# Layernorm statistics at the producers, an output projection by four tiles, a store by four tiles, and first counts ahead of the next turns, in a two-attention, two-MoE kernel on one core

## The reference

```
x = x + attn_a(layernorm(x), Wq, Wkv, Wout, bout, rel_emb)   # 16 heads of 64, one key/value head, relative bias, causal
x = x + ffn(layernorm(x), router_w, w1, b1, w2, b2)          # 8 experts, top 1, capacity 256
x = x + attn_b(layernorm(x), ...)                            # 16 heads of 8, causal, gated by a geometric score; ends in out @ out_w + out_b
x = x + ffn(layernorm(x), the same weights)
```

## Time and profile before

| | |
|---|---|
| runs | 1184.18 us median of 3 (1183.88 to 1186.83) |
| profiled execution | 1186.11 us, span 1184.40 us, mean granted PE clock 0.915 |
| PE, DVE, ACT, POOL busy | 85%, 64%, 51%, 28% of the span |
| attention A | about 36 to 583.7 us |
| moe1 | 583.9 to 665.6 us |
| b_ln, geometry, prepare_b | 665.9 to 777 us |
| attention B | 777 to 1082 us |
| out_b (`project_out`) | 1082.2 to 1093.6 us |
| moe2 | 1093.9 to 1176.5 us |
| store | to 1184.4 us |

### The profile page before, as it was taken

How to read it: one execution, slowest core, us unless ns; L and a number is a source line. 1 busy time by engine, 2 the same in 40 slices (tenths; PEclk the granted TensorE clock), 3 DMA queues, 4 the chain that set the end, 5 groups by cost and what they waited for, 6 DMA issues and landing times. The chain is left out here.

```text
span 1184.4 us, 18918 instructions
## 1 busy us (share of the span) xinstructions
PE 1006.3 (85%) x6474; PEld 651.5 (55%) x6474; DVE 761.2 (64%) x2007; ACT 598.5 (51%) x1179; POOL 328.1 (28%) x418
## 2 busy tenths in 40 slices
PE   4589999999989999999739367789999999997483
PEld 2457666676667666676439234355544445544372
DVE  5177766767567756777533599777777777763522
ACT  2477666666567666766213254314555555555120
POOL 0422112211122112210053206443443333421522
PEclk9799999999999999999959689878999999998587
DMA  5630000000000000000151100000000000000613
GB/s 176 150 88 1 1 1 1 1 2 1 1 1 1 1 1 1 1 1 1 40 175 46 46 0 1 1 1 1 1 2 1 1 2 1 1 1 3 192 56 90
DMA packets 47615, 32.40 MB, mean 27 GB/s; under 512 B 9104, under 2 KB 43680, under 8 KB 47520
## 3 DMA queue, kind: packets, MB, share of 16 engines
q1 hardware_dynamic: 45472, 26.93, 8.0%
q0 software_dynamic: 2048, 4.26, 1.1%
HBM read 21.59 MB, written 11.69 MB: 28 GB/s over the span
## 5 line engine op out<-in xcount | busy, mean ns | idle before, releaser
L891 DVE TENSOR_REDUCE attn_b_least<-attn_b_slot 128x1 f32<-128x512 f32 (+3 forms) x384 | 195.0, 552 | 64.5 <-PE attn_b_slot L809 43.8
L622 ACT ACTIVATE attn_a_prob<-attn_a_score,attn_a_m_all 128x128 f32<-128x128 f32 (+7 forms) x256 | 188.8, 740 | 65.5 <-DVE attn_a_m_all L544 62.3
L958 ACT ACTIVATE attn_b_probT<-attn_b_st 128x1024 f32<-128x1024 f32 (+1 forms) x192 | 145.2, 808 | 149.9 <-PE attn_b_st L833 148.5
L540 DVE TENSOR_REDUCE attn_a_m_far<-attn_a_score 128x1 f32<-128x512 f32 (+3 forms) x192 | 105.6, 550 | 71.7 <-PE attn_a_score L451 60.9
L463 PE MATMUL attn_a_slot<-tab,attn_a_prob 128*128 128x128 f32 x1152 | 151.6, 276 | 0.0
L807 PE MATMUL attn_b_slot<-KS,attn_b_alone 128*128 128x512 f32 (+2 forms) x384 | 147.4, 454 | 3.2 <-POOL attn_b_alone L980 2.4
L475 PE MATMUL attn_a_o<-attn_a_ptsb,Vd 128*64 128x512 f32 x288 | 142.3, 613 | 0.0
L475 PE MATMUL attn_a_o<-attn_a_ptsa,Vd 128*64 128x512 f32 x288 | 142.2, 612 | 0.0
L463 PEld LDWEIGHTS attn_a_slot<-tab,attn_a_prob 128*128 128x128 f32 x1152 | 134.3, 142 | 10.7 <-issue 3.2
L807 PEld LDWEIGHTS attn_b_slot<-KS,attn_b_alone 128*128 128x128 f32 x384 | 74.8, 205 | 86.1 <-DVE attn_b_least L891 52.5
L631 ACT ACTIVATE attn_a_ptsa<-attn_a_slot 128x512 f32<-128x512 f32 x144 | 85.7, 595 | 69.8 <-PE attn_a_slot L463 69.3
(11 more groups left out here) (223 smaller groups left out, 1857.3 us busy)
## 6 DMA issues: line engine op xcount, KB each, us to landing
moe_weights_w<-in_L_ffn_w_dram SPq DMA_DIRECT2D x32, 256.0 KB, 5.0
to_experts<-xn SPq DMA_DIRECT2D x2, 1056.0 KB, 9.0
moe_experts_xe<-to_experts SPq DMA_DIRECT2D x16, 132.0 KB, 2.6
bias_by_query_and_key<-bias_by_distance SPq DMA_DIRECT2D x2, 1024.0 KB
bias_near<-bias_by_query_and_key SPq DMA_DIRECT2D x2, 1024.0 KB, 8.1
from_experts<-xn SPq DMA_DIRECT2D x2, 1024.0 KB, 9.6
moe_experts_back<-from_experts SPq DMA_DIRECT2D x8, 256.0 KB, 3.8
moe_weights_b<-in_L_ffn_b_dram SPq DMA_DIRECT2D x16, 64.0 KB, 5.4
```

What stands on the lines that cost most here:

```text
L540: nc.vector.tensor_reduce(least, score[t % 2][:, at:at + nk - win], AX.X, ALU.min).then_inc(far_done, 1)
L622: nc.scalar.activation(probs(g)[:, j, 0:nk], score[t % 2][:, at:at + nk], ACT.Exp, bias=m_all[:, j:j + 1], scale=-1.0, accum_out=rowsum[g ...
L891: nc.vector.tensor_reduce(least[m // PER % 2][:, c, a, qt:qt + 1], bank[u % SLOTS_S][:, 0:w], AX.X, ALU.min).then_inc(slot_free, 1)
L958: nc.scalar.activation(probT[n % 2][:, two, lo:], st[:, two, lo:], ACT.Exp, scale=-1.0).then_inc(exp_done, 1)
```

## The change

Five edits. (1) `bn_stats` leaves `b_ln` and both `dispatch` phases. Each tile's statistics are made where X gets its last value: in `attention_a` behind the add with `s = 1`, in moe1's `experts` behind each chunk's four adds, in `project_out` behind each chunk's add. They go to one tile `stats` that lives through the program. Each has a wait on the add before it on the same engine. `a_ln` keeps its own. (2) `dispatch`'s parts are now eight and eight tiles, and DVE's order around the first chunk changes. (3) On PE `counts(0)` stands in front of `turn(1)`. (4) `project_out` works by chunks: four transposes into one bank, one copy, four matmuls, one add, with a buffer for each chunk; out_b is added to X by POOL inside `attention_b`, batch 0 at step 0 and batch 1 at step 12. (5) The final store is four DMAs, issued by SP inside moe2's `experts` as each chunk is updated; the last phase only waits.

```
 def dispatch(...):
-        parts = (range(0, BLK), range(BLK, TILES))
+        parts = (range(0, 2 * BLK), range(2 * BLK, TILES))
...
             turn(0)
             logits(0)
+            counts(0)
             turn(1)
-            counts(0)
...
-            statistics(range(0, BLK))
             variance(0)
             nc.vector.tensor_scalar(xn[:, :, D].bitcast(I32), spare[:, :], -(SLOTS + 1.0), None, ALU.add)
-            statistics(range(BLK, 2 * BLK))
             inverse(0)
             normal(0)
-            statistics(range(2 * BLK, TILES))
             variance(1)
+            normal(1)
+            inverse(1)
             choose(0)
-            inverse(1)
-            normal(1)
             place(0)
             normal(2)
             normal(3)
...
 def attention_a, add(g):
                 nc.vector.tensor_tensor(x, x, bank[u % SLOTS_S][:, 0:P], ALU.add).then_inc(added, 1)
+                if s:
+                    dve.wait_ge(added, g + 1)
+                    nc.vector.bn_stats(stats[:, b * QT + tile(g), :], x)
...
 def attention_b, POOL:
+                if n in (0, PER):
+                    bias_out(n // PER)
...
+            def bias_out(b):
+                mine = X[:, b * QT:(b + 1) * QT, :]
+                nc.gpsimd.tensor_tensor(mine, mine, boutb[:, :].unsqueeze(1).to_broadcast([P, QT, D]), ALU.add)
...
 def project_out(...):
+            turn(0)
+            turn(1)
+            for c in range(NC):
+                project(c)
+                if c + 2 < NC:
+                    turn(c + 2)
...
+            for c in range(NC):
+                tiles = slice(c * BLK, (c + 1) * BLK)
+                dve.wait_ge(y_done, c + 1)
+                nc.vector.tensor_tensor(X[:, tiles, :], X[:, tiles, :], y_ps[c][:, :, :], ALU.add).then_inc(summed, 1)
+                dve.wait_ge(summed, c + 1)
+                for i in range(c * BLK, (c + 1) * BLK):
+                    nc.vector.bn_stats(stats[:, i, :], X[:, i, :])
...
 def experts(...), SP:
+            if out is not None:
+                into, stored = out
+                for i in range(TILES // BLK):
+                    tiles = slice(i * BLK, (i + 1) * BLK)
+                    sp.wait_ge(updated, i + 1)
+                    sp.dma_start(into.rearrange("b (t p) d -> p (b t) d", p=P)[:, tiles, :], X[:, tiles, :]).then_inc(stored, 16)
 def experts(...), DVE:
+            for c in range(TILES // BLK):
+                dve.wait_ge(fetched[c], 16)
+                for i in range(c * BLK, (c + 1) * BLK):
+                    ins = nc.vector.scalar_tensor_tensor(X[:, i, :], back[:, i, :], gate[:, i:i + 1], X[:, i, :], ALU.mult, ALU.add)
+                ins.then_inc(updated, 1)
+                if out is None:
+                    dve.wait_ge(updated, c + 1)
+                    for i in range(c * BLK, (c + 1) * BLK):
+                        nc.vector.bn_stats(stats[:, i, :], X[:, i, :])
```

More of the change, by code:

```diff
@@ L103, in _ @@
             nc.vector.memset(xnT[:, :, 0:1], 0.0)
-            for i in range(TILES):
-                ins = nc.vector.bn_stats(stats[:, i, :], X[:, i, :])
-            link(ins)
+            if made is None:
+                for i in range(TILES):
+                    ins = nc.vector.bn_stats(stats[:, i, :], X[:, i, :])
+                link(ins)
             for i in range(TILES):
@@ L228, in wide @@
                 return x.unsqueeze(2).to_broadcast([P, BLK, E])
-            def statistics(tiles):
-                for i in tiles:
-                    ins = nc.vector.bn_stats(stats[:, i, :], X[:, i, :])
-                link(ins)
             def variance(k):
@@ L1006, in project_out, with turn @@
         block = ph.block()
-        per = (blocks + BLK - 1) // BLK
-        def part(c):
-            return range(c * BLK, min(blocks, (c + 1) * BLK))
         @block.tensor
         def _(pe):
-            def turn(i):
-                for c in range(per):
-                    n = i * per + c
-                    if n >= 4:
-                        pe.wait_ge(moved_act, n - 3)
-                    for j in part(c):
-                        ins = nc.tensor.transpose(pt[n % 4][:, (j % BLK) * P:(j % BLK + 1) * P],
-                                                  O_all[:, i, j * P:(j + 1) * P], ident[:, :])
-                    ins.then_inc(turned, 1)
-            turn(0)
-            for i in range(TILES):
-                if i + 1 < TILES:
-                    turn(i + 1)
-                pe.wait_ge(moved_act, (i + 1) * per)
-                if i >= 2:
-                    pe.wait_ge(y_used, i - 1)
-                for j in range(blocks):
-                    ins = nc.tensor.matmul(y_ps[i % 2][:, 0:P], oT[i % 2][:, j, :], w_out[:, j, :],
-                                           start=j == 0, stop=j == blocks - 1)
-                ins.then_inc(y_done, 1)
+            def turn(c):
+                for j in range(BLK):
+                    ins = nc.tensor.transpose(pt[c][:, j * P:(j + 1) * P], O_all[:, c * BLK + j, :], ident[:, :])
+                ins.then_inc(turned, 1)
@@ L1036, in _, with project @@
+            def project(c):
+                pe.wait_ge(moved, c + 1)
+                for j in range(BLK):
+                    ins = nc.tensor.matmul(y_ps[c][:, j, :], oT[c][:, j * P:(j + 1) * P], w_out[:, :], start=True, stop=True)
+                ins.then_inc(y_done, 1)
+            turn(0)
+            turn(1)
[3 more added lines that the diff above has]
+                    turn(c + 2)
         @block.scalar
         def _(act):
-            for i in range(TILES):
-                if i >= 2:
-                    act.wait_ge(y_done, i - 1)
-                for c in range(per):
-                    act.wait_ge(turned, i * per + c + 1)
-                    w = P * len(part(c))
-                    nc.scalar.activation(oT[i % 2][:, c * BLK:c * BLK + len(part(c)), :].rearrange("p j q -> p (j q)"),
-                                         pt[(i * per + c) % 4][:, 0:w], ACT.Copy).then_inc(moved_act, 1)
+            for c in range(NC):
+                act.wait_ge(turned, c + 1)
+                nc.scalar.activation(oT[c][:, :], pt[c][:, :], ACT.Copy).then_inc(moved, 1)
@@ L1047, in _ @@
         @block.vector
         def _(dve):
-            nc.vector.tensor_tensor(X[:, :, :], X[:, :, :], bias[:, :].unsqueeze(1).to_broadcast([P, TILES, D]),
-                                    ALU.add).then_inc(biased, 1)
-            dve.wait_ge(biased, 1)
-            for i in range(TILES):
-                dve.wait_ge(y_done, i + 1)
-                nc.vector.tensor_tensor(X[:, i, :], X[:, i, :], y_ps[i % 2][:, 0:D], ALU.add).then_inc(y_used, 1)
+            for c in range(NC):
+                tiles = slice(c * BLK, (c + 1) * BLK)
[4 more added lines that the diff above has]
+                    nc.vector.bn_stats(stats[:, i, :], X[:, i, :])
@@ L1229, in _ @@
                                         b2[:, e, :].unsqueeze(1).to_broadcast([P, 2, D]), ALU.add).then_inc(ye_ready, 1)
-            for i in range(TILES):
-                if i % BLK == 0:
-                    dve.wait_ge(fetched[i // BLK], 16)
-                nc.vector.scalar_tensor_tensor(X[:, i, :], back[:, i, :], gate[:, i:i + 1], X[:, i, :], ALU.mult, ALU.add)
+            for c in range(TILES // BLK):
[7 more added lines that the diff above has]
+                        nc.vector.bn_stats(stats[:, i, :], X[:, i, :])
 def geometry(nc, xnT, w_geo, sel, decay_logits, scale_row, kv_gate, gate, ident, constants, w_q, q_bias, q_scale, QS4):
```

47 lines of the change are left out of this document (24 added, 23 removed).

## The result

| | before | after |
|---|---|---|
| median of all runs, us | 1183.18 (1179.56 to 1187.64, 16 runs) | 1179.91 (1174.97 to 1181.29, 16 runs) |
| ratio to before, 95% interval | | 0.9958 (0.9943 to 0.9974) |
| profiled execution, us | 1186.11 | 1175.80 |
| its span, us; mean granted clock | 1184.4; 0.915 | 1174.0; 0.918 |

The change makes the kernel faster by 0.42%, 5.0 us at 1184 (the ratio with its interval is the comparison; the bare medians differ by 3.3). The median is another matter: put on the forecast's own scale, 1184.18 x 0.9958 is 1179.2, 4.1 above the 1175.1 given and just inside the range, whose upper end was 1179.5; the bare median of 1179.91 is 4.8 above 1175.1 and 0.4 above the range.

A forecast was written before the change was run, and what follows sets the result against it. PE was taken to bound the attentions, and chains across engines the short phases. Terms 2.6 + 2.4 − 0.3 − 0.3 − 0.1 + 0.25 + 4.5 gave 9.05 us, so 1175.1 us; range 1171.5 to 1179.5, held at 0.8.

The forecast's parts named there:

- Part 1, dispatch: First send in both dispatch phases comes 8.73 us after DVE's start instead of 11.33; gain 2.6 in moe1, 2.4 in moe2.
- Chunk 1: Rival in dispatch: the second chunk becomes the wait, its places 1.5 us late in both phases, total 1178.1; chance 0.10.
- Part 2, attention A: Statistics in attention A mostly hide in DVE's waits: at most 0.3 us for PE, the last tile's 0.28 in the open.
- Part 3: From moe1 to `b_ln`, where DVE alone works: a loss of 0.1 us, between −0.3 and +0.3.
- Part 4, out_b: In `out_b`, PE at half clock until 1088.6, then DVE bounds: gain 0.25 us; POOL's additions in attention B cost 0.
- better case: In `out_b`, the clock rises at once and DVE's four chunks end at 1092.0: +1.6 us.
- The rival of the blocked DVE: POOL's two 2.27 us additions in attention B hold up DVE's small operations: 4.5 us, total 1179.6; chance 0.03.
- Part 5, the store: At the end, last chunk's DMA issued 2.3 us earlier and landing in 2.8 instead of 5.1; gain taken as 4.5.
- the one from the sum to the median: Whole kernel: runs' median lies 1.93 us below the profiled execution, so 1184.18 less the 9.05 sum gives 1175.1.
- no idle stretch of PE grows: Argument against the rival that more half-clock PE time in experts and `out_b` makes the kernel slower, up to 1189; chance 0.04.

The follow-up runs named there:

- Counts late: The changed kernel with PE's first counts put back behind the second turn, all else kept; 1179.30 us, ratio 0.9903.
- the three short traces: Profiles of three follow-up kernels (square root's table loaded early; old `project_out`; early stores alone on the kernel before) whose attention B took 299.3 to 300.6 us.
- series 3: Third group of follow-up runs, on its own chip: the kernel before 1181.85 us, the changed kernel 1176.93 us, ratio 0.9952.
- warm PE: The changed kernel with 56 unused identity transposes at each dispatch's end and 36 ahead of each experts; 1173.92 us, ratio 0.9926.
- statistics A back: The changed kernel with attention A's 16 statistics moved out to the start of moe1's dispatch; 1172.58 us, ratio 0.9921.
- series 1 and 2: First two groups of follow-up runs, each on its own chip; the kernel before took 1191.32 us in the first, 1192.45 in the second.

## Why the prediction came out as it did

- **Part 1, dispatch: size right, reason half wrong.** 2.53 and 2.52 for 2.6 and 2.4; start of the first send 8.80 for 8.73. "`counts(0)` without the transposes" was taken as the edit that removes the 2.17 us wait. Counts late shows that DVE's order removes it alone. What the prediction overlooked is that the reordered `normal(1)` feeds PE's transposes, so that these are over when the mask comes.
- **Chunk 1:** no hole at the fifth send in any trace. The rival fell; the sum for it had taken every hand-over in full.
- **Part 2, attention A:** the mechanism right, the size 0.6 for 0.3. The instruction behind a new `bn_stats` comes 0.53 us after the add instead of 0.35:

```profile
308.61 0.29 DVE L572 TENSOR_TENSOR X<-X,attn_a_slot 128x128 f32<-128x128 f32 x1 [0.20 <-PE attn_a_slot L488]
308.93 0.29 DVE L575 BATCH_NORM_STATS2 stats<-X 128x6 f32<-128x128 f32 x1
309.14 0.28 DVE L536 CUSTOM_DVE_ANT_0 attn_a_score<-attn_a_score,bias_near 128x128 f32<-128x128 f32 x1
```

  Of the 15 adds ahead of the last, four let the next instruction start 0.10 to 0.18 us later than before, 0.58 together: those behind which DVE had stood only 0.06 to 0.14 us (the prediction counted five). Where it had stood 0.24 or more, waiting for PE, the statistics are hidden, but for one add, whose next instruction came 0.35 us later and had waited for PE. Attention A grew by 0.61. At one mean clock (0.975) it takes 546.7 to 546.8 us in the three traces without these statistics and 547.2 to 547.4 in five with them. The last tile's costs 0.32 for 0.28.
- **Part 3:** −0.33 (8.56 in nine of the eleven traces of the new form, 8.22 in two) for −0.1, a little outside the bounds given. DVE's rows show four statistics where the earlier trace rows had the next adds:

```profile
659.48 1.14 DVE L1227 SCALAR_TENSOR_TENSOR X<-moe_experts_back,gate,X 128x128 f32<-128x128 f32 x4 [7.46 <-DMA moe_experts_back<-from_experts]
660.65 0.87 DVE L1232 BATCH_NORM_STATS2 stats<-X 128x6 f32<-128x128 f32 x4
...
668.04 1.17 DVE L109 BATCH_NORM_AGGREGATE b_ln_mv<-stats 128x2 f32<-128x6 f32 x16 [0.29 <-issue]
```

- **Part 4, out_b:** a mis-sized term, +1.57 for +0.25. The step is the clock: the forecast held PE at 1.2 GHz until the second chunk's result, at 1088.6, and it was at 2.4 GHz from 1085. That the gain equals the prediction's better case (+1.6, clock up at once) is luck: in after the clock was at half for 3.4 us, and in counts late, where it was up throughout, the phase took 9.2 us, 2.8 less than before. POOL's additions cost nothing that shows:

```profile
797.07 2.36 POOL L1890 TENSOR_TENSOR X<-X,boutb 128x1024 f32<-128x1024 f32 x1
802.77 0.41 POOL L991 TENSOR_SCALAR_AFFINE_SELECT attn_b_probT<-attn_b_probT 128x256 f32<-128x256 f32 x1 [3.35 <-ACT attn_b_probT L953]
837.50 2.37 POOL L1890 TENSOR_TENSOR X<-X,boutb 128x1024 f32<-128x1024 f32 x1
840.14 0.41 POOL L991 TENSOR_SCALAR_AFFINE_SELECT attn_b_probT<-attn_b_probT 128x256 f32<-128x256 f32 x1 [0.27 <-ACT attn_b_probT L953]
```

  2.36 and 2.37 for 2.27, and the masks behind them still waited for ACT, 3.35 and 0.27 us. DVE was busy 14.44 us of the 17 around them, 14.42 before. The rival of the blocked DVE fell at these two places; DVE made only reductions of PSUM tiles while POOL added, so the rule of the Trainium skill (page "SBUF — State Buffer", section "SBUF: two separate sides") stays untested.
- **Part 5, the store:** 4.49 for 4.5.
- **The step that gave too much** is the one from the sum to the median: "the median of the runs lies 1.93 below that execution, hence 1184.18 − 9.05". It holds PE's clock fixed in everything that isn't touched. The gain in the touched stretches was larger than forecast (9.9 for 9.05), and the timed runs moved by 3.3 to 5.0 all the same. That the profiled execution came near its own forecast (1175.80 for 1177.1) is in part luck, since the untouched stretches, which move by up to 1.3 us each, nearly cancelled. "Against: no idle stretch of PE grows" was the wrong test: in attention B the second stretch at 1.2 GHz differs between executions of one program (20.5 and 17.1 us in before's two traces, 17.1, 13.7 and 17.1 in after's three), and in the three short traces it was 3.4 us or none. The pairs at equal clock and the 4 us step in attention B show the size. That this step is what put after's clock low in the first result and in series 3, and that the moved phases and not chance decide it, is argued, not shown, since only profiled runs show their windows.

What stays open: which property of a program's timing decides the clock in attention B and elsewhere, why warm PE and statistics A back were granted more, and what held the engines before the ninth send on two of the chips.

## What to carry to other kernels

Follow a moved instruction to every engine that it feeds: two edits may mend the same wait, and only taking each back alone, and both together, tells what each is worth. In a phase where engines idle in turn, a chain of rows summed with its hand-overs gave dispatch's gains to some 0.1 us; a store cut in four with each part issued as its data is complete gave 4.5 us, and nothing in the traces paid for it. Start such a stretch at the touched phase itself: counted from the program's start attention A's last add came 0.15 us earlier, yet attention A had lost 0.61, under a setup that was 0.76 shorter. For differences below 1% the time of this kernel is also its granted clock: compare runs at equal clock, or sum the touched stretches, before a difference of 5 us is believed or denied.

## What the runs showed that I had not expected

- The mean granted clock of the same program ran from 0.907 to 0.923 (before) and 0.910 to 0.926 (after), worth 6 to 7 us per 0.01.
- At the start of attention B in after, PE was busy without a hole from 798 to 808 and stayed at 1.2 GHz (0.50); it had been at 2.4 GHz (1.00) from 786 to 790, where it was busy 1.58 and 1.45 of each 2 us, and fell at 791. The Trainium skill, page "TensorE: Matmul & The Clock Gate", section "Part 1: The HAM clock gate", says that activity releases the throttle and that the number of matmuls at the lower clock varies from run to run. The traces agree with the second (in `out_b` of the three traces of after the clock rises 3.8, 4.0 and 4.9 us after attention B's end). A stretch that the profile shows busy throughout at half clock does not go with the first, if what the profile calls busy is what the page calls activity; no run here shows that, and the measurement decides.
- In series 1 and 2 every trace has some 2.4 us more in each dispatch, before the ninth send, whatever the kernel, with engines that wait for nothing the trace names.
